# Window attention scan: new score as an unnormalised sum times 1/z, maximum over the older scores, shuffled rows kept twice

## The reference

```
q_local = feature @ wq_w + wq_b
init_buf = feature[:, :64, :]
def step(buf, q_i):
    ki = concatenate([buf, zeros((B, 1, D))], axis=1)      # 65 keys, the last is zero
    scores = einsum('bwd,d->bw', q_i[:, None, :] * ki, w2_w) + w2_b[0]
    alpha = softmax(scores, axis=1)
    v_i = einsum('bwd,bw->bd', ki, alpha)
    return concatenate([buf[:, 1:, :], v_i[:, None, :]], axis=1), v_i
_, vs = scan(step, init_buf, qs)                           # 960 steps
```

## Time and profile before

| | us |
|---|---|
| median of 3 runs | 2843.85 (2842.83 to 2847.93) |
| the profiled execution | 2847.15 |
| its span in the trace | 2845.3 |
| Vector engine busy | 2248.1 (79%) |
| Scalar engine busy | 1286.1 (45%) |
| Tensor engine busy | 1189.3 (42%) |
| GpSimd busy | 287.0 (10%) |

### The profile page before, as it was taken

The page is one execution under the profiler, slowest core; times in us unless marked ns, Lnnn a source line. Parts: engine busy times, 40 slices in busy tenths (PEclk is TensorE's granted clock), DMA queues, the critical chain, the costliest instruction groups (busy, mean ns, idle before and its releaser), DMA issues. The chain is left out here.

```text
span 2845.3 us, 38133 instructions
## 1 busy us (share of the span) xinstructions
PE 1189.3 (42%) x7272; PEld 529.5 (19%) x7272; DVE 2248.1 (79%) x15205; ACT 1286.1 (45%) x3230; POOL 287.0 (10%) x425
## 2 busy tenths in 40 slices
PE   3010100001010101000003787878877877787797
PEld 1000000000000000000001111223422333233365
DVE  5999999999999999999994789776767667765233
ACT  1333333333333333333361456557855676577742
POOL 0000000000000000000010020032113210321211
PEclk9999999999999999999997799889988898799998
DMA  5000000000000000000015012103110211100100
GB/s 136 1 1 1 1 1 1 1 1 1 1 1 1 1 1 1 1 1 1 1 32 133 8 31 56 20 21 82 38 44 21 65 46 30 33 23 27 41 1 23
DMA packets 80181, 66.13 MB, mean 23 GB/s; under 512 B 8702, under 2 KB 64808, under 8 KB 79944
## 3 DMA queue, kind: packets, MB, share of 16 engines
q1 hardware_dynamic: 76872, 57.40, 8.3%
q0 software_dynamic: 3072, 6.30, 0.7%
HBM read 34.77 MB, written 28.57 MB: 22 GB/s over the span
## 5 line engine op out<-in xcount | busy, mean ns | idle before, releaser
L1310 DVE TENSOR_REDUCE nm_half<-pair 128x2 f32<-128x1024 f32 x512 | 611.6, 1220 | 196.7 <-PE pair L1558 178.4
L204 ACT ACTIVATE ex<-row,nmax 128x65 f32<-128x65 f32 x960 | 336.1, 350 | 924.2 <-DVE nmax L306 837.6
L1198 ACT ACTIVATE pt<-pair 128x1024 f32<-128x1024 f32 x512 | 513.6, 1025 | 382.7 <-PE pair L1568 368.1
L264 DVE SCALAR_TENSOR_TENSOR junk<-ex,tab 128x65 f32<-128x65 f32 x2850 | 622.1, 219 | 1.4 <-issue 0.4
L367 PE MATMUL p_s<-tab,bdg 128*128 128x32 f32 x120 | 31.9, 406 | 829.4 <-DVE tab L269 829.4
L1534 PE MATMUL p_o<-pt,va 128*9 128x512 f32 x2048 | 298.4, 658 | 7.0 <-ACT pt L1198 7.0
L269 DVE TENSOR_TENSOR tab<-raw,rz 128x1 f32<-128x1 f32 (+1 forms) x1890 | 286.6, 152 | 3.2 <-issue 1.1
L298 DVE SCALAR_TENSOR_TENSOR junk<-ex,rz,row 128x65 f32<-128x65 f32 x930 | 265.5, 285 | 3.0 <-issue 2.7
L1558 PE MATMUL pair<-ks,qs 48*128 48x512 bf16 x1024 | 209.5, 420 | 111.7 <-ACT pt L1198 55.8
L264 DVE DVE_READ_ACCUMULATOR junk<-ex,tab 128x1 f32 x2850 | 236.8, 83 | 0.2
L1568 PE MATMUL pair<-qs,ks 50*128 50x512 bf16 x1024 | 210.8, 415 | 52.6 <-ACT pt L1198 22.1
(11 more groups left out here) (254 smaller groups left out, 1951.1 us busy)
## 6 DMA issues: line engine op xcount, KB each, us to landing
parts_dram<-parts SPq DMA_DIRECT2D x48, 256.0 KB, 3.5
qs<-parts_dram SPq DMA_DIRECT2D x32, 192.0 KB, 4.7
ks<-parts_dram SPq DMA_DIRECT2D x32, 192.0 KB, 5.2
hid<-xs_dram SPq DMA_DIRECT2D x33, 128.0 KB, 2.1
ys_dram<-hid SPq DMA_DIRECT2D x33, 128.0 KB, 1.8
h_dram<-f SPq DMA_DIRECT2D x20, 128.0 KB, 2.5
x<-in_x SPq DMA_DIRECT2D x4, 512.0 KB, 8.3
w_W<-in_W SPq DMA_DIRECT2D x1, 2048.0 KB
```

Of the source, the lines that this page charges most:

```text
L204: nc.scalar.activation(ex[:, r % 2, :], row[:, r % 2, 1:], ACT.Exp, bias=nmax[:, r % 2:r % 2 + 1], accum_out=z[:, r % 2:r % 2 + 1]).then_i ...
L264: nc.vector.scalar_tensor_tensor(junk[:, g, :], ex[:, k, :], 1.0, tab[:, g, r:r + ROW], ALU.mult, ALU.mult, accum_out=raw[:, g:g + 1]).the ...
L1198: nc.scalar.activation(pt[:, kt % 2, :, tokens(t)], pair[fill.pair][:, :, :], ACT.Exp, scale=SCALE).then_inc(s_exp, 1)
L1310: nc.vector.reduce_max(nm_half[:, t, hp % 2, :, q], pair[fill.pair][:, :, :], AX.X, negate=True)\
```

## The change

The new score is summed with the unnormalised weights into `raw[3]`, and multiplied by 1/z in a small operation of its own. The maximum is taken over the scores that are there before the new one; where the oldest key alone stood out, the new score could lie above it, and `CAP` then limits the weights and 1/z. Each shuffle writes the row twice, 65 scores from column r on and 65 from column r + 1 on: the sum and the maximum read the first copy, the exponential the second, into whose place 63 the new score is written. The exponential waits for the maximum and for the new score. `normalised` (a tensor_tensor) becomes `divided` (a scalar_tensor_tensor with max and mult). The division of `raw[1:3]` moves from the end of the step to the start of the next, ahead of the reciprocal; the shuffle is the last operation of a step.

```diff
-        row = sb("row", [P, 2, ROW + 1])
+        row = sb("row", [P, 2, 2, ROW])
...
                     act.wait_ge(s_max, L * c + r + 1)
-                    nc.scalar.activation(ex[:, r % 2, :], row[:, r % 2, 1:], ACT.Exp, bias=nmax[:, r % 2:r % 2 + 1],
+                    if r:
+                        act.sem_inc(s_pace_act, 1)
+                        act.wait_ge(s_new, (L - 1) * c + r)
+                    nc.scalar.activation(ex[:, r % 2, :], row[:, r % 2, 1, :], ACT.Exp, bias=nmax[:, r % 2:r % 2 + 1],
...
-                nc.vector.scalar_tensor_tensor(junk[:, g, :], ex[:, k, :], 1.0, tab[:, g, r:r + ROW], ALU.mult,
+                nc.vector.scalar_tensor_tensor(junk[:, g, :], ex[:, k, :], CAP, tab[:, g, r:r + ROW], ALU.min,
                                                ALU.mult, accum_out=raw[:, g:g + 1]).then_inc(done, 1)
-            def normalised(g0, g1, k, r, done):
-                nc.vector.tensor_tensor(tab[:, g0:g1, r + WIN:r + ROW], raw[:, g0:g1].unsqueeze(2),
-                                        rz[:, k:k + 1].unsqueeze(1).broadcast_to((P, g1 - g0, 1)),
-                                        ALU.mult).then_inc(done, 1)
+            def divided(to, g0, g1, k, done):
+                nc.vector.scalar_tensor_tensor(to, rz[:, k:k + 1].unsqueeze(1).broadcast_to((P, g1 - g0, 1)),
+                                               1.0 / CAP, raw[:, g0:g1].unsqueeze(2), ALU.max, ALU.mult)\
+                    .then_inc(done, 1)
+            def coefficients(c, r):
+                dve.wait_ge(s_raw, 2 * (L * c + r) + 2)
+                divided(tab[:, 1:3, r + WIN:r + ROW], 1, 3, r % 2, s_coef)
+            def shifted(q, r):
+                src = tab[:, 0, r:r + ROW]
+                pair = bass.AP(src.tensor, src.offset, [src.ap[0], [1, 2], [1, ROW]])
+                nc.vector.stream_shuffle(row[:, q % 2, :, :], pair, [q] * L).then_inc(s_row, 1)
+            def largest(c, r):
+                dve.wait_ge(s_row, L * c + r + 1)
+                nc.vector.reduce_max(nmax[:, r % 2:r % 2 + 1], row[:, r % 2, 0, 1:], AX.X, negate=True)\
+                    .then_inc(s_max, 1)
...
-                nc.vector.stream_shuffle(row[:, 1, :], tab[:, 0, 0:ROW + 1], [1] * L).then_inc(s_row, 1)
+                shifted(1, 0)
...
                     dve.wait_ge(s_exp, n + 1)
+                    if r:
+                        coefficients(c, r - 1)
                     nc.vector.reciprocal(rz[:, k:k + 1], z[:, k:k + 1]).then_inc(s_rz, 1)
                     if not last:
+                        dve.wait_ge(s_row, n + 2)
+                        nc.vector.scalar_tensor_tensor(junk[:, 3, :], ex[:, k, :], CAP, row[:, 1 - k, 0, :], ALU.min,
+                                                       ALU.mult, accum_out=raw[:, 3:4]).then_inc(s_raw_new, 1)
+                        largest(c, r + 1)
                         weighted(0, k, r, s_raw_score)
-                        dve.wait_ge(s_row, L * c + r + 2)
+                        dve.wait_ge(s_raw_new, m)
+                        dve.sem_inc(s_pace, 1)
                         dve.wait_ge(s_rz, n + 1)
-                        nc.vector.scalar_tensor_tensor(junk[:, 3, :], ex[:, k, :], rz[:, k:k + 1],
-                                                       row[:, 1 - k, 0:ROW], ALU.mult, ALU.mult,
-                                                       accum_out=row[:, 1 - k, WIN:ROW]).then_inc(s_new, 1)
+                        divided(row[:, 1 - k, 1, WIN - 1:WIN].unsqueeze(2), 3, 4, k, s_new)
                     if r:
                         dve.wait_ge(s_coef, n)
                     weighted(1, k, r, s_raw)
                     if not last:
-                        dve.wait_ge(s_new, (L - 1) * c + r + 1)
-                        nc.vector.reduce_max(nmax[:, 1 - k:2 - k], row[:, 1 - k, 1:], AX.X, negate=True)\
-                            .then_inc(s_max, 1)
-                        dve.wait_ge(s_raw_score, (L - 1) * c + r + 1)
-                        normalised(0, 1, k, r, s_score)
+                        dve.wait_ge(s_raw_score, m)
+                        divided(tab[:, 0:1, r + WIN:r + ROW], 0, 1, k, s_score)
                     weighted(2, k, r, s_raw)
                     if r < L - 2:
-                        dve.wait_ge(s_score, (L - 1) * c + r + 1)
+                        dve.wait_ge(s_score, m)
                         dve.sem_inc(s_pace, 1)
-                        nc.vector.stream_shuffle(row[:, k, :], tab[:, 0, r + 1:r + 2 + ROW], [r + 2] * L)\
-                            .then_inc(s_row, 1)
-                    dve.wait_ge(s_raw, 2 * n + 2)
-                    normalised(1, 3, k, r, s_coef)
+                        shifted(r + 2, r + 1)
+                    if last:
+                        coefficients(c, r)
```

More of the change, by code:

```diff
@@ L40 @@
 EPS = 1e-5
+CAP = 1e30
 def window_attention(nc, io, xt, w, stacks, s_weights, moe_dram):
@@ L87, in window_attention @@
         junk = sb("junk", [P, 4, ROW])
-        raw = sb("raw", [P, 3])
+        raw = sb("raw", [P, 4])
         pf = ps("pf", [P, 2, 4 * P])
@@ L110, in window_attention @@
                                                    sem("s_new"), sem("s_coef"))
[L111 removed]
+        s_raw, s_raw_score, s_score, s_raw_new = sem("s_raw"), sem("s_raw_score"), sem("s_score"), sem("s_raw_new")
         s_clear = sem("s_clear")
@@ L278, in _ @@
                 dve.sem_inc(s_pace, 1)
-                nc.vector.stream_shuffle(row[:, 0, 1:], tab[:, 0, 0:ROW], [0] * L).then_inc(s_row, 1)
-                nc.vector.stream_shuffle(row[:, 1, :], tab[:, 0, 0:ROW + 1], [1] * L).then_inc(s_row, 1)
+                nc.vector.stream_shuffle(row[:, 0, 1, :], tab[:, 0, 0:ROW], [0] * L).then_inc(s_row, 1)
+                shifted(1, 0)
                 dve.wait_ge(s_row, L * c + 1)
-                nc.vector.reduce_max(nmax[:, 0:1], row[:, 0, 1:], AX.X, negate=True).then_inc(s_max, 1)
+                nc.vector.reduce_max(nmax[:, 0:1], row[:, 0, 1, :], AX.X, negate=True).then_inc(s_max, 1)
                 dve.wait_ge(s_bdc, c + 1)
@@ L288, in _ @@
                 for r in range(L):
-                    k, n = r % 2, L * c + r
+                    k, n, m = r % 2, L * c + r, (L - 1) * c + r + 1
                     last = r == L - 1
                     dve.wait_ge(s_exp, n + 1)
+                    if r:
+                        coefficients(c, r - 1)
                     nc.vector.reciprocal(rz[:, k:k + 1], z[:, k:k + 1]).then_inc(s_rz, 1)
                     if not last:
+                        dve.wait_ge(s_row, n + 2)
+                        nc.vector.scalar_tensor_tensor(junk[:, 3, :], ex[:, k, :], CAP, row[:, 1 - k, 0, :], ALU.min,
+                                                       ALU.mult, accum_out=raw[:, 3:4]).then_inc(s_raw_new, 1)
+                    if not last:
+                        largest(c, r + 1)
+                    if not last:
                         weighted(0, k, r, s_raw_score)
-                        dve.wait_ge(s_row, L * c + r + 2)
+                    if not last:
+                        dve.wait_ge(s_raw_new, m)
+                        dve.sem_inc(s_pace, 1)
                         dve.wait_ge(s_rz, n + 1)
-                        nc.vector.scalar_tensor_tensor(junk[:, 3, :], ex[:, k, :], rz[:, k:k + 1],
-                                                       row[:, 1 - k, 0:ROW], ALU.mult, ALU.mult,
-                                                       accum_out=row[:, 1 - k, WIN:ROW]).then_inc(s_new, 1)
+                        divided(row[:, 1 - k, 1, WIN - 1:WIN].unsqueeze(2), 3, 4, k, s_new)
                     if r:
```

## The result

The changed kernel takes 2805.39 us (median of 4 runs, 2802.15 to 2813.75) against 2843.34 before: ratio 0.987, 95% interval 0.9848 to 0.9892. It is faster by 1.3%, where I had forecast 0.7% slower. The profiled execution took 2813.75 us, its span is 2812.0. It is the longest of the four, 8.4 us above the median, while the profiled execution before lies 3.8 above its own (2847.15 and 2843.34), so the two traces differ by less than the medians, 33.3 us and not 38.

The account below looks back on a forecast made before the run. The Scalar engine loop binds at 1.36 us a step, after the change the Vector engine at 1.375; 13.5 us for 900 steps, 1.2 for blocks and 4 for stalls make 18.7, giving 2862 us, range 2822 to 2892.

Parts of the forecast that it names:

- What bounds, before and after: Scan step: loop through the Scalar engine binds before at 1.36 us, the Vector engine after at 1.375.
- the engine's own 1.31: Step of the kernel before: the Vector engine by itself would need 1.31 us, leaving 0.05 slack.
- The loop after the change, 1.26: Changed step: loop from coefficient division through new score's division and exponential needs 1.26 us, alone giving 0.10 a step.
- The Vector engine's sum, 1.375: Changed step: the Vector engine's start-to-start distances add up to 1.375 us, above the loop's 1.26 and above 1.36.
- weighted(0) 0.20: Changed step: weighted(0) hands over after 0.20 us, as before, because the same double wait follows; bounds 0.15 and 0.20.
- rival B: Wait behind weighted(0) hidden by longer operations ahead and the queue's lead; step 1.325, time 2817 us; chance 0.17.
- my argument against B: Behind weighted(2) the gap is there though a division and a weighted sum stand ahead of it.
- the sum of the new score: Changed step, Vector engine: 0.13 us where it was 0.21, the per-partition scalar read gone.
- The row's wait: New score's sum awaits the row just shuffled, 0.33 us; the engine comes at 0.355, so free by 0.025.
- The block's net: Block start 0.066 us longer, block end 0.03 won: some 0.04 a block, 1.2 us in all.
- The stalls: Scan steps stalling for no listed reason: 2 us more from longer instruction stream, some 2 more from lost slack.
- The rule on semaphores: Trainium skill's "Minimize op count, not sems": wait behind weighted(0) would be free, sum 1.325; forecast held the trace against it.

Follow-up runs that it names:

- hoisted_no_counter: Kernel before, with the row's wait moved ahead of weighted(0) and no counter increment ahead of the shuffle: 2760.8 us, ratio 0.970.
- once_no_counter: Changed kernel with the row shuffled once, no separate wait at the new score's division, no counter increment ahead of the shuffle: 2704.3 us, ratio 0.952.
- no_counter_shuffle: Changed kernel without the counter increment ahead of the shuffle, the wait for the score kept: 2720.8 us, ratio 0.958.

## Why the prediction was wrong

**What bounds, before and after: right.** The loop binds before. That the slack behind it is small is right too, but the engine's own 1.31 contained two exposed separate waits, 0.07 ahead of the new score and 0.09 ahead of the shuffle, as if they were work.

**The loop after the change, 1.26:** the timeline gives 602.22 - 601.66 to the division, 0.15, 0.03 and 0.47, together 1.21 or 1.22; without the increment ahead of the shuffle it bound at 1.220. The 0.04 is the same term, weighted(0), 0.06 less, and 0.01 more for the sum.

**The Vector engine's sum, 1.375: one term failed.** The step measured 1.310. The term is "weighted(0) 0.20 ... I keep 0.20, since the pattern is the same"; it measured 0.141. That is 0.06 of the 0.065 between sum and measurement, 54 us in 900 steps. Between the two profiled executions the forecast was +18.7 us and -33.4 came, a miss of 52: 58.5 from the step, less 5 for stalls and 3 for block ends and step 1 that turned out dearer; some 2 more came from ahead of the scan. So the step alone would have missed by more than the whole did.

The pattern was not the same, because another result is awaited. Before, the separate instruction waits for the reciprocal, which ends 0.04 before it, and L298 has to follow by 0.076. In the change it waits for the raw sum and starts 0.15 before the engine is free for the division, of which 0.108 suffices. The experiments show it from both sides: the wait put on the operation itself gave 0.07 before, and the maximum moved away from between sum and division cost 0.09 in the change.

I had named the right outcome as rival B and gave it 0.17. Its mechanism was right in part: the maximum ahead of weighted(0) is what hides the wait. But B said that the queue needs longer operations to run ahead, and the records don't show that. At the three places with a separate wait (ahead of L298, of the new score's division and of the shuffle) it starts 0.038 or 0.039 after the end of the awaited operation in nine steps of ten, before as after, so the queue had got there and stood waiting each time. What counts is how old the awaited result is. This also answers my argument against B, the gap behind weighted(2): there the score division is awaited, which ends only 0.06 before weighted(2)'s accumulator read starts (602.23 + 0.15 = 602.38 and 602.44 in the earlier trace rows), and the mask can't be loaded until 0.154 after its end. In the earlier trace rows weighted(2) is stretched to 0.34, the result is older, and the gap is gone. Not tried was the direct test, the kernel before with its two waits changed over, so that L298 carries the one for rz.

**The other terms:** the sum of the new score 0.142 for 0.13; the reciprocal and the three divisions 0.07 each, as the tensor_tensor; the shuffle 0.205 and weighted(2) with mask 0.26, as forecast. The 12 ns of the sum are outweighed by 20 ns on the reciprocal, the new score's division and weighted(1). The row's wait didn't bite.

**Block ends and stalls.** The block's net was forecast at 0.04 and measured at 0.0 (the turn +0.13, step 30 -0.13), step 1 added 0.11 that I hadn't foreseen. The stalls grew by 9 us, not 4.

**The rule on semaphores.** The page "VectorE: DVE Perf Modes" of the Trainium skill holds, in its section "The DRAIN you can't avoid", that a semaphore after each copy costs nothing extra, and in its rules that the count of operations matters. Here a separate wait or increment cost 0.07 to 0.09 us at three places and nothing at one; the measurement decides. By the rule the step would have been 1.325 and the time 2817, near the measured 1.310 and 2805. That is luck: the wait is free here because its result is old, and the rule would have called it free before the change too, where it cost 0.07.

## What to carry to other kernels

On an engine that runs operations of 0.07 to 0.2 us, a wait that needs an instruction of its own is part of the budget when its result is fresh. Here the next operation could start 0.11 to 0.15 us after the end of what such an instruction awaited, and 0.03 to 0.05 after it where the operation carried the wait itself. So let the operation carry the fresh wait, move the wait that is satisfied long before to an earlier instruction that has none, or put other work between the result and its use. Before shortening a loop, take such gaps out of both the loop and the other engine's work; only then do the two lengths say which edits pay. And an operation added to get something off the loop (the second copy of the row, 65 us) is paid in full once the bound has moved; look for an order of readers and writer that makes it needless.

## What the runs showed of the hardware

A wait in an instruction of its own: it starts 0.038 us after the end of the awaited operation, and what follows it starts no sooner than 0.076 us after its start (L298, 930 steps), 0.108 (the new score's division, behind a wait with an increment) or 0.114 (the mask's loading, likewise). Increments in a row start 0.093 to 0.098 apart.

Stalls without a listed reason come to 24.9 us in the scan of the changed kernel, the longest 0.36, and to 31.7 us with two counters more. In hoisted_no_counter, where the Vector engine has some 0.17 us of slack a step, they are 0.2 us. They go with the number of instructions that the Vector engine's queue has in a step, the separate ones counted: 0.2 us at 14, 1.6 and 8.7 at 15, 8.7 and 16 at 16, 9.6 to 20.8 at 17, about 25 at 18, 31.7 at 20, each from a single profiled execution. The slack plays a part as well: once_no_counter and no_counter_shuffle have the same step of 1.220 and 8.7 and 20.8 us of stalls.

They also go with the packets of the instruction queue. In the changed kernel both come about every 9.4 us, and each of its 137 stalled steps starts less than 2.5 us ahead of such a packet, as 28% of random moments do. A packet of 8.2 KB for 7 steps of 18 instructions is some 64 bytes an instruction, an estimate. That the stalls are fetches of instructions is strongly suggested by this; no run tested it by itself.

The granted clock of TensorE was 0.50 all through the scan of the changed kernel, the level of 1.2 GHz, and 1.00 in the earlier trace rows, 2.4 GHz. The 622 matmuls of the scan were busy 123.83 us at the one and 123.89 us at the other, with ends that the profile models. In 13 executions of the kernel before on one chip, the four with a mean granted clock of 0.95 took 2842.4 us in the mean and the nine with 0.69 took 2838.1. So the higher clock gains nothing here, and a difference of that size is a small part of the result's 38 us. Why those executions are longer is open.
